# Alternating the small products of variance and gate with the convolution taps on TensorE

## What is computed

```python
def conv(x, w): ...            # sign(pad(x)) * sign(w), VALID
y = ln_c(x)
h = relu(bn1(conv(y, w1)))
x = x + relu(bn2(conv(h, w2)) + y)
t = to_tokens(x)
n = ln_t(t)
top_probs, top_idx = top_k(softmax(n @ gate_w + gate_b), 2)   # renormalised
hidden = silu(n @ w1[e]) * (n @ w2[e])
t = t + sum(dispatch[e] * (hidden @ w3[e]))
```

## Time and profile before

| | us |
|---|---|
| median of three runs | 498.39 |
| profiled execution | 498.73 |
| its span, first to last instruction | 496.8 |
| TensorE busy | 450.0 (91%) |
| VectorE busy | 439.4 (88%) |
| ScalarE busy | 408.7 (82%) |
| GpSimd busy | 295.5 (59%) |
| all taps, L813, 192 matmuls, sum of durations | 52.3 |
| all variance products, L829, 256 matmuls, sum of durations | 31.3 |

### The profile page before, as it was taken

The page is one execution under the profiler, slowest core; times in us unless marked ns, Lnnn a source line. Parts: engine busy times, 40 slices in busy tenths (PEclk is TensorE's granted clock), DMA queues, the critical chain, the costliest instruction groups (busy, mean ns, idle before and its releaser), DMA issues.

```text
span 496.8 us, 14231 instructions
## 1 busy us (share of the span) xinstructions
PE 450.0 (91%) x4186; PEld 384.2 (77%) x4186; DVE 439.4 (88%) x1248; ACT 408.7 (82%) x949; POOL 295.5 (59%) x380
## 2 busy tenths in 40 slices
PE   7998989999997627899999999999999999999972
PEld 6676767777774515798988988989899899998871
DVE  3776897997979998899998999999999999999973
ACT  5797878887885413899999999999999999999960
POOL 3200018777777777777777766666555555547571
PEclk9898979989987765999999999999999999999997
DMA  6993102022000024420223432224441525310054
GB/s 163 152 391 134 42 2 70 27 73 71 27 32 28 31 52 90 91 66 28 53 51 72 86 76 56 58 63 104 95 108 42 149 57 142 94 33 21 20 177 169
DMA packets 62664, 40.97 MB, mean 82 GB/s; under 512 B 50003, under 2 KB 54318, under 8 KB 62080
## 3 DMA queue, kind: packets, MB, share of 16 engines
q1 hardware_dynamic: 52784, 29.30, 23.8%
q0 software_dynamic: 8800, 8.94, 5.3%
q10 hardware_dynamic: 1008, 1.84, 1.0%
HBM read 21.46 MB, written 19.19 MB: 82 GB/s over the span
## 4 chain that ended last, share of the span: by engine, by line
PE 51%; DVE 30%; ACT 8%; issue 5%; DMA 3%; SPq 1%; POOL 1%; DVEq 0%; POOLq 0%; ACTq 0%
PE up L982 9%; PE up L984 8%; PE up L813 6%; PE turn L995 6%; DVE xs_lo L1530 4%; PE small L829 4%; ACT xc L713 4%; PE lines L1017 4%; DVE hidden L1604 3%; PE small L963 3%; DVE hidden L1609 2%; PE up L788 2%; DVE sq L1604 2%; PE up L799 2%; PE lines L1019 2%
## 5 line engine op out<-in xcount | busy, mean ns | idle before, releaser
L532 POOL DMA_INDIRECT results<-result,page_in x147 | 156.5, 1064 | 88.1 <-ACT xc L713 39.7
L515 POOL DMA_INDIRECT pages<-payload,slot_int x128 | 130.6, 1021 | 95.3 <-DVE slot_int L1431 57.5
L982 PE MATMUL up<-up_w,xs_hi 128*128 x588 | 139.0, 276 | 7.4 <-DVE xs_lo L1530 6.7
L984 PE MATMUL up<-up_w,xs_lo 128*128 x588 | 138.4, 275 | 0.0
L713 ACT ACTIVATE xc<-up,back_scales 128x512 f32<-128x512 f32 x147 | 107.8, 733 | 12.6 <-PE up L984 10.7
L982 PEld LDWEIGHTS up<-up_w,xs_hi 128*128 128x128 f16 x588 | 57.9, 98 | 19.0 <-issue 12.2
L1614 DVE TENSOR_TENSOR hidden_lo<-turn,hidden_hi 128x512 f16<-128x512 f32 x98 | 67.5, 688 | 1.6 <-ACT hidden_hi L726 0.6
L726 ACT ACTIVATE hidden_hi<-turn 128x512 f16<-128x512 f32 x98 | 65.1, 664 | 0.5 <-PE turn L995 0.5
L1604 DVE SCALAR_TENSOR_TENSOR hidden<-up,page_in,xc 128x128 f32<-128x128 f32 x196 | 59.4, 346 | 6.2 <-ACT xc L713 5.4
L984 PEld LDWEIGHTS up<-up_w,xs_lo 128*128 128x128 f16 x588 | 58.1, 99 | 5.4
L995 PE MATMUL turn<-ident,hidden 128*128 128x128 f32 x392 | 58.8, 273 | 0.0
(11 more groups left out here) (265 smaller groups left out, 978.4 us busy)
## 6 DMA issues: line engine op xcount, KB each, us to landing
pages<-x SPq DMA_DIRECT2D x4, 1332.0 KB, 11.1
page_in<-pages SPq DMA_DIRECT2D x147, 36.0 KB
page_in<-pages SPq DMA_DIRECT2D x147, 32.0 KB
x_in<-in_x SPq DMA_DIRECT2D x7, 512.0 KB, 4.4
out<-up_raw SPq DMA_DIRECT2D x5, 512.0 KB, 3.1
results<-result,page_in POOLq DMA_INDIRECT x147
up_raw<-in_L_ffn_w SPq DMA_DIRECT2D x4, 512.0 KB, 8.1
pages<-payload,slot_int POOLq DMA_INDIRECT x128, 2.2
```

Of the source, the lines that this page charges most:

```text
L515: pool.indirect_dma_start(out=pages, out_offset=bass.IndirectOffsetOnAxis(ap=slot_int[q % PAYLOADS][:, t:t + 1], axis=0), in_=payload[q % ...
L532: pool.indirect_dma_start(out=results, out_offset=bass.IndirectOffsetOnAxis(ap=page_in[g % LOADS][:, k, D + AT_TOKEN:D + AT_TOKEN + 1].bit ...
L982: pe.matmul(target, xs_hi[g % 2][:, k * P:(k + 1) * P], weights[:, bass.ds(e * 2, 2 * HID)], start=True, stop=False)
L984: last = pe.matmul(target, xs_lo[g % 2][:, k * P:(k + 1) * P], weights[:, bass.ds(e * 2, 2 * HID)], start=False, stop=True)
```

## The change

The products of variance(1, b) now stand between the taps of conv(0, 1, s), those of the gate between the taps of conv(1, 0, s), and those of variance(0, a) between the taps of conv(0, 0, a), which for that moves ahead of count(r). After each tap stand one or two products (1, 1, 2, 1, 1, 2). The waits of both halves come ahead of the first tap. This is so in t = 2 to 8 for the first two and t = 1 to 7 for the last; where only one half exists it is as before. On VectorE conv2 of the first half moves ahead of places(r).

```diff
+            def variance_in_conv(n, q, which, c, conv_q):
+                conv_waits(which, c, conv_q)
+                variance_waits(n, q)
+                for t in range(len(TAPS)):
+                    tap(which, c, t)
+                    for j in range(t * TILES // 2 // len(TAPS), (t + 1) * TILES // 2 // len(TAPS)):
+                        square_mean(n, j)
+
+            def gate_in_conv(q, which, c, conv_q):
+                conv_waits(which, c, conv_q)
+                gate_waits(q)
+                for t in range(len(TAPS)):
+                    tap(which, c, t)
+                    for j in range(t * TILES // 2 // len(TAPS), (t + 1) * TILES // 2 // len(TAPS)):
+                        scores(j)
...
-                if 0 <= b < PAIRS:
-                    if t == 3:
-                        pe.wait_ge(weights_made, WM_LARGEST + 1)
+                if t == 3:
+                    pe.wait_ge(weights_made, WM_LARGEST + 1)
+                if 0 <= b and s < PAIRS:
+                    variance_in_conv(1, b, 0, 1, s)
+                elif 0 <= b < PAIRS:
                     variance(1, b)
-                if 0 <= s < PAIRS:
+                elif 0 <= s < PAIRS:
                     conv(0, 1, s)
...
-                if 0 <= b < PAIRS:
-                    if b == 0:
-                        pe.wait_ge(gate_in, 48)
+                if 0 <= b and s < PAIRS:
+                    gate_in_conv(b, 1, 0, s)
+                    conv(1, 1, s)
+                elif 0 <= b < PAIRS:
                     gate(b)
-                if 0 <= s < PAIRS:
+                elif 0 <= s < PAIRS:
                     for c in range(CH):
                         conv(1, c, s)
...
                     variance(0, a)
+                    conv(0, 0, a)
+                elif a < PAIRS:
+                    variance_in_conv(0, a, 0, 0, a)
                 if r >= 0:
                     if r == 0:
                         pe.wait_ge(tables_made, 10)
                     count(r)
-                if a < PAIRS:
-                    conv(0, 0, a)
...
+                if 0 <= s < PAIRS:
+                    conv2(0, s)
                 if 0 <= r < PAIRS:
                     places(r)
                 if 0 <= s < PAIRS:
-                    for c in range(CH):
-                        conv2(c, s)
+                    conv2(1, s)
                     for c in range(CH):
                         residual(c, s)
```

More of the change, by code:

```diff
@@ L801, in center2, with conv_waits @@
                 last.then_inc(centered2, 1)
-            def conv(which, c, q):
+            def conv_waits(which, c, q):
                 if which == 0:
@@ L810, in conv, with tap, variance_waits @@
                     pe.wait_ge(conv1_read, CH * (q + 1))
[L811 to L818, removed]
+            def tap(which, c, t):
+                i, j = TAPS[t]
+                product = pe.matmul(cv[c], conv_w[:, which, t, :],
+                                    (sign1, sign2)[which][:, c * ROWS + i:(c + 1) * ROWS + i, j:j + W],
+                                    start=(t == 0), stop=(t == len(TAPS) - 1))
+                if t == len(TAPS) - 1:
+                    product.then_inc((conv1_ready, conv2_ready)[which], 1)
+            def conv(which, c, q):
+                conv_waits(which, c, q)
+                for t in range(len(TAPS)):
+                    tap(which, c, t)
+            def variance_waits(n, q):
                 pe.wait_ge((squared, squared2)[n], CH * (q + 1))
@@ L827, in variance, with square_mean @@
                         pe.wait_ge(gate_read, q)
+            def square_mean(n, j):
+                product = pe.matmul(var_ps[n][:, 2 * j:2 * j + 2], sq[:, j * P:(j + 1) * P], mean_col[:, :],
+                                    start=True, stop=True)
+                if j == TILES // 2 - 1:
+                    product.then_inc((var_ready, var2_ready)[n], 1)
+            def variance(n, q):
+                variance_waits(n, q)
                 for j in range(TILES // 2):
-                    last = pe.matmul(var_ps[n][:, 2 * j:2 * j + 2], sq[:, j * P:(j + 1) * P], mean_col[:, :],
-                                     start=True, stop=True)
-                last.then_inc((var_ready, var2_ready)[n], 1)
+                    square_mean(n, j)
             def norm(c, q):
@@ L853, in turn_channels, with gate_waits, scores @@
                 last.then_inc(turned_ready, 1)
+            def gate_waits(q):
+                if q == 0:
+                    pe.wait_ge(gate_in, 48)
+                pe.wait_ge(var2_read, q + 1)
+            def scores(j):
+                product = pe.matmul(gate_ps[:, j * 2 * E:(j + 1) * 2 * E], xc2[:, j * P:(j + 1) * P],
+                                    gate_mat[:, :, :].rearrange("p a e -> p (a e)"), start=True, stop=True)
+                if j == TILES // 2 - 1:
+                    product.then_inc(gate_ready, 1)
             def gate(q):
-                pe.wait_ge(var2_read, q + 1)
+                gate_waits(q)
                 for j in range(TILES // 2):
-                    last = pe.matmul(gate_ps[:, j * 2 * E:(j + 1) * 2 * E], xc2[:, j * P:(j + 1) * P],
-                                     gate_mat[:, :, :].rearrange("p a e -> p (a e)"), start=True, stop=True)
-                last.then_inc(gate_ready, 1)
+                    scores(j)
+            def variance_in_conv(n, q, which, c, conv_q):
+                conv_waits(which, c, conv_q)
+                variance_waits(n, q)
+                for t in range(len(TAPS)):
+                    tap(which, c, t)
+                    for j in range(t * TILES // 2 // len(TAPS), (t + 1) * TILES // 2 // len(TAPS)):
+                        square_mean(n, j)
+            def gate_in_conv(q, which, c, conv_q):
+                conv_waits(which, c, conv_q)
+                gate_waits(q)
+                for t in range(len(TAPS)):
+                    tap(which, c, t)
+                    for j in range(t * TILES // 2 // len(TAPS), (t + 1) * TILES // 2 // len(TAPS)):
+                        scores(j)
             def turn_chosen(q):
```

8 lines of the change are left out of this document (4 added, 4 removed).

## The result

| | before | after |
|---|---|---|
| median, us | 498.4 | 505.1 (503.7 to 506.9) |
| ratio | 1 | 1.014 [1.010, 1.018] |
| profiled execution, its span | 498.7, 496.8 | 504.5, 502.6 |
| TensorE busy | 450.0 | 443.4 |
| VectorE, ScalarE busy | 439.4, 408.7 | 439.8, 407.0 |

The account below looks back on a forecast made before the run. TensorE and VectorE were both taken as nearly full in the convolution steps, VectorE setting the stage's end. Step terms summed to +2.55 us: 501.3 on the profiled scale, 500.9 median; own range 499 to 503, with rivals 496.8 to 505.0.

Parts of the forecast that it names:

- the cost of a run: One alternating run on TensorE at full clock: 2.65 us against 3.03 before, bounds 2.40 and 3.03, saving 0.38.
- The step to a tap: Inside an alternating run, going from the last gate product to a tap: 0.06 us, five or six times, counted as 0.25.
- read as several loads: Rival, chance 0.08: both weight loads of a product hide, a run takes 1.95 us, and the time is 491.8.
- The gate's wait for the sign: TensorE ahead of the gate's run: a new stall of 0.75 us until ScalarE's last sign of the first convolution.
- scores to logarithm: Pair a's variance run waits for VectorE's second-convolution read: 4.35 us from scores to logarithm; before, 3.50 (t = 5), 4.23 (t = 6).
- logarithm to x_ln: From pair a's logarithm to x_ln: 2.68 us, before 3.65 in t = 6; norm's earlier place gains 0.95.
- One sign did not come: Listed as showing the forecast right: VectorE's wait before x_ln in t = 6, 1.83 us before, would be gone.
- the gain in t = 6 and 7: Scores to end of x_ln in t = 6: 8.32 us, before 9.17, so -0.85; the same for t = 7.
- is hidden under this wait: In t = 3 the gate waits for signs delayed by a 1.99 us weight conversion, hiding the clock's fall; scores +1.75 us.
- a rival with a chance of 0.10 and a time of 506.5: New waits lower the clock in steps that had it full: +5.6 us, in t = 3 and t = 5 to 7.
- VectorE has no wait that the order could fill: Reason given for t = 8 and later: the change adds 0 there.
- Move with the end of the stage; I give no credit: GpSimd's sixteen scatters of each pair begin in t = 4, about 2 us later; no credit was given for them.

## Why the prediction was right and wrong

**Right: the cost of a run and the new waits.** Forecast 2.65 us, measured 2.59, in the bounds of 2.40 and 3.03. One load hides, the other is paid, as the earlier trace rows had it. The step to a tap, 0.06 taken five or six times, is 0.30 to 0.36 and not 0.25, so the forecast's own terms give about 2.75; the run shows 0.03 (0.14 less the paid load of 0.11). What the Trainium skill (TensorE: Matmul & The Clock Gate, Part 2) says of loads pulled ahead, read as several loads, would have given 1.95, and no run here shows it. The gate's wait for the sign (forecast 0.75, measured 0.62 in t = 5), scores to logarithm (4.35; 4.40 in t = 6), logarithm to x_ln (2.68; 2.83) are as forecast, and t = 4 (+0.65; +0.35) nearly. t = 1 and 2 together were forecast at +1.0 and measured at +1.15. One sign did not come: VectorE's wait before x_ln in t = 6, which was to go, is 1.01 us, and with the variance of pair a plain it is 1.01 too.

**Wrong: the base of the gain in t = 6 and 7.** The forecast takes off 0.85 in each, from the 3.65 us between logarithm and x_ln, and gives them to the order. Measured were -0.7 and -0.4, so the numbers nearly held; the reason did not, and that they came near was luck: both steps had a fall in the kernel before and none in the changed one's trace. The earlier trace rows come from a step in which a fall had made TensorE late. Without a fall the old order needs 3.00 us and the step 18.30; the new one needs 2.83 and 19.0. So the change loses 0.7 in each full step, and it gains only against steps that a fall had slowed. This term was mis-sized by 0.8 (0.95 against 0.17), and it hid that the run of pair a is a loss in every step from t = 2 to 7, which the experiments show to be the largest part.

**Wrong: the fall in t = 3 "is hidden under this wait".** On TensorE, ScalarE and VectorE of the changed kernel in t = 3, in order of time:

```profile
45.88 0.39 PE L814 MATMUL up<-sign,conv_w 128*128 128x512 bf16 x1 [0.26 <-DVE largest L1237]
...
49.91 1.95 PE L866 MATMUL turn<-ident,xc 128*128 128x128 f32 x8
50.08 0.28 ACT L582 ACTIVATE log_var<-small,both_eps 128x16 f32<-128x16 f32 x1 [3.61 <-PE small L837]
50.51 1.99 ACT L652 ACTIVATE up_w<-up_raw,scales 128x2048 f16<-128x2048 f32 x1
...
51.65 2.91 PE L788 MATMUL up<-x_in,center_mat 128*128 128x256 f32 x8
54.52 0.63 ACT L602 ACTIVATE sign<-branch 128x512 bf16<-128x512 f32 x1
55.21 0.39 PE L814 MATMUL up<-sign,conv_w 128*128 128x512 bf16 x1 [0.65 <-ACT sign L602]
...
58.03 0.42 DVE L1344 TENSOR_TENSOR logits<-small,rstd 128x256 f32<-128x256 f32 x1 [3.96 <-PE small L875]
```

The run began at 45.88 and ended at 49.91, 4.03 us instead of 2.65, and the logarithm that starts the forecast's chain came 4.20 behind the step's start instead of 2.97. The wait hides what stands between the run and the gate, not the run in front of the chain. The scores stood 12.15 us behind the start, forecast 11.05.

**Wrong: falls behind the new waits, priced at nothing in the sum.** They were a rival with a chance of 0.10 and a time of 506.5. In t = 5 the clock fell at 104.9 us, in the run of pair a behind its wait for VectorE; the step grew by 1.8, forecast 0.85. (It came in the changed kernel's second trace too, and not in the one with the results put sooner, where that step took 19.0.) In t = 8 the forecast was 0, "VectorE has no wait that the order could fill". TensorE in t = 8, in order of time, in the changed kernel; then its granted clock from 156.10 to 161.10:

```profile
152.68 1.07 PE L866 MATMUL turn<-ident,xc 128*128 128x128 f32 x8
156.09 0.61 PE L814 MATMUL up<-sign,conv_w 128*128 128x512 bf16 x1 [2.34 <-ACT sign L602]
...
161.10 2.37 PE L814 MATMUL up<-sign,conv_w 128*128 128x512 bf16 x6
161.32 0.42 DVE L1344 TENSOR_TENSOR logits<-small,rstd 128x256 f32<-128x256 f32 x1 [1.64 <-PE small L875]
```

```profile
156.10:161.10 5.00, 5.00 (x23) 4.45 (x24) 3.37 (x11) 1.75 (x8) 3.93 (x4) 0.50 0.09 31
```

In t = 8 there is no pair left to centre, so 1.73 us of cover are gone; TensorE waits 2.34 for the signs instead of 0.75, and the run behind that wait goes at 0.50, 5.0 us instead of 2.59. The kernel before has half the clock in t = 8 too, but behind the gate's products (149.77 to 151.74), so that they and the scores do not feel it:

```profile
152.40:155.70 3.30, 3.30 (x9) 1.19 (x8) 3.20 (x10) 1.75 (x8) 2.69 (x3) 0.50 0.11 36
```

The forecast had costed the steps with three pairs in flight and not the last one. The scores came 1.84 later in the step; whether that reaches the end, the runs with step 8 plain leave open.

**Half right: GpSimd.** "Move with the end of the stage; I give no credit" holds for the profiled execution, where TensorE had no wait for pages. But it was treated as a follower, and it is a bound of its own: from the first slots, 5.3 us later, through the eighth result to the tenth group of pages. It is what took back the first stage's gain in the trace with the variance of pair a plain; those with the gate or the variance of pair b plain show no wait for pages.

**The sum.** Against 2.55 forecast: t = 2 +0.55 more, t = 3 +1.05, t = 5 +0.95, t = 6 and 7 +0.6, the slots behind t = 7 +2.5; t = 0, 1 and 4 -0.9; behind the last slots -1.5. Together 5.8, the difference of the spans. The range ended at 505.0: it left out the upper half of the rival whose mechanism took part.

**Still open:** why the fall of t = 3 is longer. It lasted 6.8 us or more in ten of the eleven profiled executions with the run of pair a, and in one of the eight without it; the eleventh had a further fall in t = 2. That is an association, and no run separates what in it does this. Open too is where the two runs of pair b lose their 0.5%: with them alone the steps t = 5 to 7 take 18.2 to 18.3 us, and t = 5 of the kernel before, at full clock too, took 18.4.

## What to carry to other kernels

A gain read as the difference of two orders must be taken from a step in which nothing else was late: here the row that gave 0.95 us for the new place of norm came from a step with a fall of the clock, and without it the gain was 0.17. When small work is threaded into large work, both inherit the later of the two waits; look for the step in which the producer of that wait is least covered, the last one of a pipeline above all, and price the clock behind each new idle stretch. And before a stage's gain or loss is carried to the end, follow every queue that works without a gap, here GpSimd's: moving eight results ahead in it was worth 0.6%, more than anything the alternation brought.

## What the runs showed of the hardware

The falls of the clock do not belong to the program alone. Two kernels that differ only in the order of GpSimd's queue behind 220 us had, in t = 3 and 4, first this, then that (the variance of pair a plain, without and with the results put sooner; they ran on different chips):

```profile
42.30:63.40 21.10, 17.29 (x128) 14.33 (x128) 17.04 (x51) 16.74 (x32) 0.00 (x0) 1.00 0.08 26
63.40:83.60 20.20, 17.20 (x126) 13.95 (x126) 18.94 (x58) 17.57 (x38) 9.27 (x8) 1.00 0.12 38
```

```profile
43.00:66.00 23.00, 20.54 (x128) 17.14 (x128) 17.09 (x51) 16.78 (x32) 0.00 (x0) 0.85 0.08 24
66.00:88.10 22.10, 20.00 (x126) 16.91 (x126) 18.99 (x57) 17.62 (x37) 9.52 (x9) 0.85 0.10 37
```

The same instructions ran at a full clock in one and with a fall in each step in the other, and the two steps took 3.8 us more. The changed kernel itself took 23.2 and 22.8 us for them in one execution, with a fall in each, and 24.1 and 20.9 in its second trace, where t = 4 had none. A single trace therefore shows one draw of these falls, and a term of 1 to 2 us that rests on where a fall stood in it is uncertain by as much.
